# One bf16 mask for two uses, and f16 halves in the dense steps of x: a graph network kernel of two layers

## The reference, cut to what matters

```python
# x: 4096 x 256 f32, adj: 4096 x 4096 int32 (about 0.2% ones), neigh: 4096 x 256
mask = adj > 0
# layer 0
agg = mask @ x / max(sum(mask, 1), 1)
out = relu(concat(x @ W_self + b_self, agg @ W_nb + b_nb) @ W_comb + b_comb)
x = layernorm(x + out)
# layer 1
neib_att = tanh(neigh @ Wn1 + bn1) @ Wn2 + bn2      # hidden width 32
value    = neigh @ Wv + bv                          # width 128
x_att    = tanh(x @ Wx1 + bx1) @ Wx2 + bx2
ws  = softmax(where(mask, leaky_relu(x_att @ neib_att.T, 0.01), -9e15), axis=1)
out = concat(x @ Wfx + bfx, ws @ value)
return layernorm(x + out)
```

## Time and profile before

| | |
|---|---|
| median of three runs | 796.03 us |
| profiled execution | 795.35 us, span 793.5 us |
| TensorE matmul / weight load busy | 761.6 us (96%) / 640.6 us (81%) |
| VectorE, ScalarE, GpSimd busy | 593.4 us (75%), 561.1 us (71%), 295.0 us (37%) |
| chain that ended last, by engine | TensorE 90%, VectorE 3%, ScalarE 3% |
| DMA, mean share of 16 engines | queue of SyncE 45.9% |
| mean granted clock of TensorE | 0.993 |

### The profile page before, as it was taken

The page is one execution under the profiler, slowest core; times in us unless marked ns, Lnnn a source line. Parts: engine busy times, 40 slices in busy tenths (PEclk is TensorE's granted clock), DMA queues, the critical chain, the costliest instruction groups (busy, mean ns, idle before and its releaser), DMA issues.

```text
span 793.5 us, 20199 instructions
## 1 busy us (share of the span) xinstructions
PE 761.6 (96%) x7440; PEld 640.6 (81%) x7440; DVE 593.4 (75%) x1481; ACT 561.1 (71%) x1046; POOL 295.0 (37%) x368
## 2 busy tenths in 40 slices
PE   5999979999999999999999999999999999999885
PEld 4565758888888888888888888888888888888664
DVE  4875467778777787777777777777777787877784
ACT  2454247777777778777777777777777777777995
POOL 0031433344444433333444444333334444443101
PEclk9989999999999999999999999999999999999999
DMA  8954754544544444545445445454455444420000
GB/s 270 356 134 109 197 141 139 147 123 139 125 136 140 131 133 135 127 138 147 130 133 145 122 134 142 126 141 123 133 146 140 128 141 129 132 61 16 14 9 14
DMA packets 107404, 103.64 MB, mean 131 GB/s; under 512 B 74665, under 2 KB 88873, under 8 KB 107305
## 3 DMA queue, kind: packets, MB, share of 16 engines
q1 hardware_dynamic: 106944, 102.33, 45.9%
q10 hardware_dynamic: 360, 0.01, 0.0%
HBM read 81.34 MB, written 4.19 MB: 108 GB/s over the span
## 4 chain that ended last, share of the span: by engine, by line
PE 90%; DVE 3%; ACT 3%; issue 2%; POOL 1%; DMA 1%; SPq 0%; POOLq 0%; ACTq 0%; DVEq 0%
PE ps_v L974 20%; PE ps_agg L940 13%; PE ps_agg L937 13%; PE ps_t L961 13%; PE ps_agg L992 7%; PE ps_s L952 7%; PE ps_x L1012 3%; PE ps_x L1009 2%; PE ps_s L851 2%; PE ps_v L859 2%; PE ps_x L1018 2%; PE ps_t L842 1%; PE ps_x L868 1%; PE ps_agg L982 1%; DVE late L623 1%
## 5 line engine op out<-in xcount | busy, mean ns | idle before, releaser
L762 ACT ACTIVATE score<-ps_s,sc 128x512 f32<-128x512 f32 x256 | 178.0, 695 | 93.9 <-PE ps_s L952 90.0
L937 PE MATMUL ps_agg<-x,mask_t 128*128 128x257 f16 x1024 | 240.5, 273 | 0.0
L623 DVE TENSOR_TENSOR late<-ps_t,late 128x512 f16<-128x512 f32 x256 | 174.5, 682 | 85.3 <-ACT late L775 85.1
L577 DVE CUSTOM_DVE_ANT_0 score<-score,bias 128x512 f32<-128x512 f32 x256 | 191.1, 747 | 60.2 <-ACT score L762 60.1
L940 PE MATMUL ps_agg<-x,mask_t 128*128 128x256 f16 x1024 | 235.4, 273 | 0.0
L974 PEld LDWEIGHTS ps_v<-v,late 128*128 128x128 f16 x3072 | 191.7, 98 | 47.5 <-DVE late L623 13.7
L974 PE MATMUL ps_v<-v,late 128*128 128x128 f16 x3072 | 213.6, 219 | 7.6 <-DVE late L623 6.6
L775 ACT CAST late<-ps_t 128x512 f16<-128x512 f32 x256 | 147.8, 577 | 15.9 <-PE ps_t L961 15.7
L961 PE MATMUL ps_t<-ident,score 128*128 128x128 f32 x1024 | 155.7, 275 | 2.0 <-ACT score L769 1.8
L769 ACT ACTIVATE score<-score,exp_bias 128x1024 f32<-128x1024 f32 x128 | 146.5, 1145 | 0.8 <-DVE exp_bias L586 0.7
L388 POOL TENSOR_SCALAR mv<-mv 128x1 f32<-128x1 f32 x32 | 8.5, 265 | 370.0 <-DVE mv L608 370.0
(11 more groups left out here) (108 smaller groups left out, 734.4 us busy)
## 6 DMA issues: line engine op xcount, KB each, us to landing
adj_sb<-in_adj_dram SPq DMA_DIRECT2D x128, 512.0 KB, 4.0
neigh_sb<-in_L_gnn_neigh_dram SPq DMA_DIRECT2D x8, 512.0 KB, 7.9
score<-in_x_dram SPq DMA_DIRECT2D x8, 512.0 KB, 9.5
x_in<-in_x_dram SPq DMA_DIRECT2D x32, 128.0 KB, 3.7
out_dram<-out_sb SPq DMA_DIRECT2D x32, 128.0 KB, 3.9
mask_t<-mask SPq DMA_TRANSPOSE x128, 2.4
bias<-in_L_gnn_W_comb_dram SPq DMA_DIRECT2D x1, 512.0 KB, 9.4
bias<-in_L_gnn_W_self_dram SPq DMA_DIRECT2D x1, 256.0 KB, 7.0
```

The lines of the kernel that those rows point to most:

```text
L577: dve.tensor_tensor_reduce(score[:, b % 2, part], score[:, b % 2, part], bias[:, b % BIAS_BUFS, part], 1.0, -3.0e38, ALU.add, ALU.max, par ...
L623: dve.tensor_tensor(p_lo[:, k % 2, :], ps_t[k % 2][:, :], p_hi[:, k % 2, :], ALU.subtract).then_inc(p_lo_made, 1)
L762: act.activation(score[:, b % 2, k * GW:(k + 1) * GW], ps_s[k % 2][:, :], ACT.Prelu, alpha=SLOPE, scale=score_scale).then_inc(leaky_made, 1)
L937: mm = pe.matmul(agg[:, 0:D + 1], mask_t8[:, b % 2, c // 2, c % 2, :], x16[:, c, 0:D + 1], start=(c == 0), stop=(c == NC - 1), skip_group_ ...
```

## The change

- One mask in bf16, four buffers, serves both uses: 1.0 where there is no edge and 1.5 x 2^-121 where there is one. The low byte of the second reads as 2.0 in fp8, that of the first as zero; masked_scores subtracts the mask from scores that are kept in a large unit (score_unit). exp takes that unit as a pointer scale. GpSimd's make_bias is gone.
- Each quarter of the transpose has twice the bytes, x rows are loaded singly, and mask_t has one buffer of the same size: a quarter's transpose waits for the aggregation of the same quarter of the block before. Masks are made in slots -6, -5, -2, -1 of a block.
- x1 is stored as two f16 halves (x1_high on ScalarE, x1_low on VectorE), wx1 and wfx too; hidden and fx are six f16 matmuls each, with 96 columns of weights for hidden (three copies of wx1). tanh is written twice (f32 and f16, 96 rows), tanh_low makes the low part, x_attention is one f16 matmul with 96 x 96 weights.
- The new steps take two slots, so scores, row_max, turn, weigh and layer1 stand two slots later. The weights are scaled and split on VectorE in slots 1 to 10.

```diff
-MASK_AT = -5
-BIAS_AT = 3
+MASK_SLOTS = (-6, -5, -2, -1)
@@
-HIDDEN_AT = 17
-XATT_AT = 18
-STACK_AT = 19
-SCORE_AT = 20
-ROW_MAX_AT = 28
-TURN_AT = 30
-WEIGH_AT = 31
-LAYER1_AT = 39
+X1_LOW_AT = 17
+HIDDEN_AT = 18
+TANH_AT = 19
+XATT_AT = 20
+STACK_AT = 21
+SCORE_AT = 22
+ROW_MAX_AT = 30
+TURN_AT = 32
+WEIGH_AT = 33
+LAYER1_AT = 41
@@
-        mask = sb("mask", [P, 2, N], U8)
-        bias = sb("bias", [P, BIAS_BUFS, N], BF16)
-        mask_t = sb("mask_t", [P, 2, NC // 2, P], BF16)
+        mask = sb("mask", [P, MASK_BUFS, N], BF16)
+        mask_t = sb("mask_t", [P, NC, P], BF16)
@@ turn_mask
-                at_least(sp, agg_done, NQ * (b - 2) + q + 1)
-                sp.dma_start_transpose(mask_t[:, b % 2, q * CQ:(q + 1) * CQ, :],
-                                       mask_pairs[:, b % 2, q * QW // 2:(q + 1) * QW // 2]).then_inc(mask_t_in[q], 16)
+                at_least(sp, agg_done, NQ * (b - 1) + q + 1)
+                sp.dma_start_transpose(mask_t[:, q * CQ:(q + 1) * CQ, :],
+                                       mask[:, b % MASK_BUFS, q * QW:(q + 1) * QW]).then_inc(mask_t_in[q], 16)
@@ make_mask
-                dve.tensor_scalar(mask[:, b % 2, q * QW:(q + 1) * QW], adj_sb[:, q, :], 0.0, float(EDGE),
-                                  ALU.is_gt, ALU.mult).then_inc(mask_made, 1)
+                dve.tensor_scalar(mask[:, b % MASK_BUFS, q * QW:(q + 1) * QW], adj_sb[:, q, :], 0.0, EDGE,
+                                  ALU.is_le, ALU.add).then_inc(mask_made, 1)
@@
-            def make_bias(b, q):
...
@@ masked_scores
-                dve.wait_ge(bias_made, NQ * b + k // 2 + 1)
-                dve.tensor_tensor_reduce(score[:, b % 2, part], score[:, b % 2, part], bias[:, b % BIAS_BUFS, part],
-                                         1.0, -3.0e38, ALU.add, ALU.max,
+                dve.wait_ge(mask_made, NQ * b + k // 2 + 1)
+                dve.tensor_tensor_reduce(score[:, b % 2, part], score[:, b % 2, part], mask[:, b % MASK_BUFS, part],
+                                         1.0, -3.0e38, ALU.subtract, ALU.max,
@@
+            def x1_low(b):
+                dve.wait_ge(x1_hi_made, b + 1)
+                dve.scalar_tensor_tensor(out=x1_t[:, 1, :], in0=ps_x[:, 0:D], scalar=X1_SCALE, in1=x1_t[:, 0, :],
+                                         op0=ALU.mult, op1=ALU.subtract).then_inc(x1_lo_made, 1)
+            def tanh_low(b):
+                dve.wait_ge(tanh_made, 2 * b + 2)
+                part = slice(2 * H, H3)
+                dve.tensor_tensor(tanh16[part, :], tanh32[part, :], tanh16[part, :],
+                                  ALU.subtract).then_inc(tanh_split, 1)
@@ exps
-                act.activation(part, part, ACT.Exp, bias=exp_bias[:, b % 2:b % 2 + 1],
+                act.activation(part, part, ACT.Exp, bias=exp_bias[:, b % 2:b % 2 + 1], scale=score_unit,
@@ x_tanh
-                act.activation(tanh_sb[:, :], ps_x[0:H, 2 * P:3 * P], ACT.Tanh,
-                               bias=bx1_sb[:, 0:1]).then_inc(tanh_made, 1)
+                for out in (tanh32, tanh16):
+                    act.activation(out[:, :], ps_x[0:H3, 2 * P:3 * P], ACT.Tanh, bias=bx1_sb[0:H3, 0:1],
+                                   scale=h1_inv[0:H3, :]).then_inc(tanh_made, 1)
@@ hidden_and_fx
-                for dc in range(DC):
-                    pe.matmul(ps_x[0:H, 2 * P:3 * P], wx1_sb[:, dc, :], x1_t[:, dc * P:(dc + 1) * P],
-                              start=(dc == 0), stop=(dc == DC - 1))
-                for dc in range(DC):
-                    mm = pe.matmul(ps_x[:, 3 * P:4 * P], x1_t[:, dc * P:(dc + 1) * P], wfx_sb[:, dc, :],
-                                   start=(dc == 0), stop=(dc == DC - 1))
+                for k, (dc, (w, r)) in enumerate(product(range(DC), HI_LO)):
+                    pe.matmul(ps_x[0:H3, 2 * P:3 * P], wx1_16[:, dc, w, :], x1_t[:, r, dc * P:(dc + 1) * P],
+                              start=(k == 0), stop=(k == 3 * DC - 1))
+                for k, (dc, (r, w)) in enumerate(product(range(DC), HI_LO)):
+                    mm = pe.matmul(ps_x[:, 3 * P:4 * P], x1_t[:, r, dc * P:(dc + 1) * P], wfx16[:, dc, w, :],
+                                   start=(k == 0), stop=(k == 3 * DC - 1))
@@ x_attention
-                pe.matmul(ps_x[0:H3, 0:P], wx2_sb[:, :], tanh_sb[:, :], start=True, stop=True).then_inc(xatt_done, 1)
+                pe.matmul(ps_x[0:H3, 0:P], wx2_16[:, :], tanh16[:, :], start=True, stop=True).then_inc(xatt_done, 1)
```

More of the change, by code:

```diff
@@ L1 @@
 from contextlib import ExitStack
+from itertools import product
 import concourse.bass as bass
@@ L6 @@
 F32, F16, BF16, F8 = mybir.dt.float32, mybir.dt.float16, mybir.dt.bfloat16, mybir.dt.float8e4
-I32, U32, U8 = mybir.dt.int32, mybir.dt.uint32, mybir.dt.uint8
+I32, U32 = mybir.dt.int32, mybir.dt.uint32
 ALU = mybir.AluOpType
@@ L28 @@
 X_ONE, X_LO = D, D + 2
-BIG = 2.0 ** 100
-EDGE, EDGE_F8 = 64, 2.0
+EDGE = 1.5 * 2.0 ** -121
+EDGE_F8 = 2.0
+SCORE_BITS = 33
+MIN_SCORE_UNIT = 2.0 ** 8
 SLOPE = 0.01
@@ L36 @@
 TINY = 2.0 ** -100
+X1_SCALE = 2.0 ** 8
 TR = 4
@@ L164, in gnn_kernel @@
         tops = sb("tops", [P, 2, NT], F32)
-        early = bias[:, :, :].rearrange("p a n -> p (a n)").bitcast(F32)
+        early = mask[:, 2:4, :].rearrange("p a n -> p (a n)").bitcast(F32)
         ws_raw = early[:, 0:512].rearrange("p (c n) -> p c n", c=DC)
+        b_wide = early[:, 0:512].rearrange("p (c n) -> p c n", c=2 * DC)
         wn_raw = early[:, 512:1024].rearrange("p (c n) -> p c n", c=DC)
@@ L346, in _ @@
             for s in range(0, SLOTS + 3):
[L347 to L352, removed]
+                for q, at in enumerate(MASK_SLOTS):
+                    if (d := due(s, at, 0)) and d[0] > 0:
+                        turn_mask(d[0], q)
+                        if d[0] + 1 < NB:
+                            load_adj(d[0] + 1, q)
                 if d := due(s, LAYER0_AT + 1, 0):
@@ new lines, in scale_x_attention @@
+                wide = wx2_16[:, :].rearrange("p (k h) -> p k h", k=3)
+                scale_link(dve.tensor_copy(wide, wx2_sb[0:H3, :].unsqueeze(1).broadcast_to((H3, 3, H))))
+                part = slice(H, 2 * H)
+                dve.tensor_tensor(wide[part], wx2_sb[part, :].unsqueeze(1).broadcast_to((H, 3, H)), wide[part],
+                                  ALU.subtract).then_inc(x1_w_split, 1)
+                dve.tensor_scalar(bx2_sb[:, :], bx2_sb[:, :], s_xn[:, 0:1], None, ALU.mult).then_inc(bounds_scaled, 1)
@@ new lines, in split_fx, with split_wx1 @@
+            def split_fx():
+                scale = w_scale[:, 0:1]
+                scale_link(dve.tensor_scalar(wfx16[:, :, 0, :], wfx_sb[:, :, :], scale, None, ALU.mult))
+                dve.scalar_tensor_tensor(out=wfx16[:, :, 1, :], in0=wfx_sb[:, :, :], scalar=scale, in1=wfx16[:, :, 0, :],
+                                         op0=ALU.mult, op1=ALU.subtract).then_inc(x1_w_split, 1)
+            def split_wx1(c):
+                scale = w_scale[:, 1:2]
+                wide = wx1_16[:, c].rearrange("p v (k h) -> p v k h", k=3)
+                thrice = wx1_sb[:, c, :].unsqueeze(1).broadcast_to((P, 3, H))
+                scale_link(dve.tensor_scalar(wide[:, 0], thrice, scale, None, ALU.mult))
+                dve.scalar_tensor_tensor(out=wide[:, 1], in0=thrice, scalar=scale, in1=wide[:, 0], op0=ALU.mult,
+                                         op1=ALU.subtract).then_inc(x1_w_split, 1)
@@ L568, in first_part @@
                     scale_x_attention()
+                if s == 3:
+                    x1_weight_bounds()
+                if s == 5:
+                    scale_x1_weights()
+                if s == 7:
+                    split_fx()
+                if s in (8, 10):
+                    split_wx1((s - 8) // 2)
                 if s == Z_BIAS_SLOT:
@@ L617, in add_fx @@
                 dve.wait_ge(resx_made, b + 1)
-                dve.tensor_tensor(res[:, b % RES_BUFS, 0:DV], ps_x[:, 3 * P:4 * P], res[:, b % RES_BUFS, 0:DV],
-                                  ALU.add).then_inc(res_made, 1)
+                dve.scalar_tensor_tensor(out=res[:, b % RES_BUFS, 0:DV], in0=ps_x[:, 3 * P:4 * P], scalar=fx_inv,
+                                         in1=res[:, b % RES_BUFS, 0:DV], op0=ALU.mult, op1=ALU.add).then_inc(res_made, 1)
             def p_low(b, k):
@@ L654, in _ @@
                     masked_scores(*d)
+                if d := due(s, X1_LOW_AT, 0):
+                    x1_low(d[0])
+                if d := due(s, TANH_AT, 0):
+                    tanh_low(d[0])
                 if d := due(s, LAYER1_AT - 1, 0):
@@ L665, in _ @@
                     add_fx(d[0])
-                if d := due(s, MASK_AT):
-                    if d[0] > 0 and d[1] % 2 == 0:
-                        make_mask(d[0], d[1] // 2)
+                for q, at in enumerate(MASK_SLOTS):
+                    if (d := due(s, at, 0)) and d[0] > 0:
+                        make_mask(d[0], q)
                 if d := due(s, TURN_AT):
@@ L788, in normalise2, with x1_high @@
```

(8 more changed lines are left out.)

112 lines of the change are left out of this document (64 added, 48 removed).

## The result

| | before | after |
|---|---|---|
| median of the runs | 796.0 us | 769.15 us (768.72 to 770.73) |
| ratio | 1 | 0.9658, interval 0.9642 to 0.9673 |
| profiled execution, span | 795.35, 793.5 us | 770.73, 768.9 us |
| one block of the loop | 21.753 us | 20.889 us |

The kernel became 3.4% faster.

The account below looks back on a forecast made before the run. TensorE was taken as the bound: 28 blocks x 0.66 = -18.5 us, with once-only terms +1.6, +1.2, -3.3 and +1.5, sums to -17.5. Forecast 778.5 us, range 767 to 792.

Parts of the forecast that it names:

- Removed work: TensorE, each block: dropping f32 hidden and fx saves 1.20 us and f32 x_attention 0.48, together 1.68.
- Added work: TensorE, each block: f16 matmuls for fx 0.34, hidden 0.50, x_attention 0.08; sum 0.92 us, between 0.73 and 1.11.
- The rival of cheap narrow loads: TensorE's loop: 96-column loads are cheap and nothing stalls, 28 x 0.95 = 26.6 us saved, total 770.5; chance 0.11.
- No gaps: TensorE, hidden's 96-column weights: no loss where the weight shape changes; bounds nothing to 0.36 us a block.
- The stall: TensorE before slot 1's weighing, waiting for p_low or layer1: 0.1 us a block, range 0 to 0.6.
- this chain as a rival: Slot 1's chain becomes the bound: stall 0.5 instead of 0.1 us a block, total 790; chance 0.13.
- The GpSimd pass is hidden in the steady part, so its removal brings nothing there: Steady loop: removing GpSimd's mask pass was given no gain.
- The mask write keeps its pace: VectorE's mask write, 0.70 us, keeps its shape with bf16 output; over 0.8 us would make the prediction wrong.
- the slower rival: VectorE's mask write slows with bf16 output, each taking 0.6 us more: total 812 us; chance 0.06.
- The hole at 102 us: Head, TensorE's wait for the mean: 2.4 us less stall plus half the clock's 1.7, together -3.3 us.
- The first transpose: Start of the run: doubled data lands later and stalls TensorE 0.7 to 1.9 us, taken as +1.2.
- The tail: After the last aggregate: two more slots +3.8 us, exp's pointer scale with the second tanh +1.5.

Follow-up runs that it names:

- experiment 1: The changed kernel with hidden, fx and x_attention back in f32, mask, slots and buffers as changed: 795.91 us, ratio to before 0.9971, block 21.842 us.
- 3 and 4: The changed kernel with hidden's weights at 32 and at 64 columns instead of 96 from block 1 on: 775.51 and 776.21 us.
- experiment 2: The changed kernel with a GpSimd pass over each mask quarter back in its old odd slots from block 1, result unused: 799.54 us, ratio to before 1.0025.
- experiment 9: The changed kernel with the unused GpSimd pass over all four mask quarters put in slot 2, behind norm2: 773.79 us, ratio to before 0.9709.
- experiment 5: The changed kernel run once more, unaltered: 769.33 us, ratio to before 0.9655, block 20.889 us.
- experiment 8: The changed kernel with a constant instead of a pointer scale in exp, which leaves out the masking: 765.42 us, ratio to before 0.9612.
- experiment 6: The changed kernel with row_scale one slot earlier, in VectorE's slot 7 ahead of the mask: 765.85 us, ratio to before 0.9609.

## Why the prediction was right, and where not

**Removed work, right.** With the dense steps in f32 the block is 0.953 longer (experiment 1 against after). The 1.68 read from the earlier trace rows less the 0.728 measured as added is 0.952.

**Added work, the term that was mis-sized.** The prediction put a matmul with 96 columns at 0.083, the middle between an f16 row and an f32 row; it starts its successor after 0.056, like one with 128. Seven of them are 0.19 too dear a block, 28 blocks 5.3 us, most of the 6.1. The rival of cheap narrow loads, given 0.11, had this term right. That it came within 1.4 us of the time is in part luck: it saves 26.6 in the loop where 24.6 came, and too little in the head. The load record is longer, 123 against 98 ns, but it lies behind the running matmul:

```profile
L1073 PEld LDWEIGHTS ps_x<-x_t,wx 128*96 128x96 f16 x192 | 14.4, 123 | 1.7 <-DVE x_t L657 1.4
L1076 PEld LDWEIGHTS ps_x<-wfx,x_t 128*128 128x128 f16 x192 | 12.1, 98 | 0.0
```

TensorE: Matmul & The Clock Gate in the Trainium skill, Weight-path perf modes, keeps the fast load for 128 columns. The record agrees, the pace doesn't show it.

**No gaps, right**, and experiments 1, 3 and 4 show what they would have cost.

**The stall, right in size, wrong in place.** 0.1 was taken and 0.096 came, but not before slot 1's weighing. The size is partly luck: it was a guess in a range of 0 to 0.6. The argument from the earlier trace rows followed VectorE alone and stopped at layer1; the chain goes on through ScalarE's exp to slot 2's turn. The prediction named this chain as a rival at 0.5 of stall. It was right that it is the next bound: experiment 2 shows it at 0.92.

**"The GpSimd pass is hidden in the steady part, so its removal brings nothing there": failed.** It was true of the kernel before, where TensorE never waits, and experiment 1, without the pass, gains nothing in the loop. In the new slots it is not: there the pass, at the places that experiment 2 gives it, costs 0.92. The prediction had one half of the reason in hand. It moved hidden out of slot 1 and found the 1.20 us of cover gone, but it did not ask what the pass would cost there, and so what its removal is worth, nor what norm2's move would do to the order on GpSimd. In the new slots neither part was worth much without the other (795.91 us without the f16 products, 799.54 with the pass); together they are worth 27 us. That the whole 27 would have been missed with make_bias itself in the new slots is not shown, since the stand-in need not wait as make_bias did.

**The mask write keeps its pace, right:** 702 ns on average, so the slower rival had no ground.

```profile
L486 DVE TENSOR_SCALAR mask<-adj_sb 128x1024 bf16<-128x1024 int32 x128 | 89.6, 702 | 1.1 <-issue 0.2
L622 DVE CUSTOM_DVE_ANT_0 score<-score,mask 128x512 f32<-128x512 f32 x256 | 176.2, 688 | 18.7 <-ACT score L822 17.2
```

The mean of masked_scores fell from 747 to 688 ns: the ones that met a pass are gone.

**The hole at 102 us, right, and too cautious.** The wait is 0.78 instead of 2.94, 2.2 for the 2.4 taken. The granted clock from 100 to 120 us went from 0.91 to 1.00 altogether, where the prediction gave back one half of 1.7. The stretch also holds the dense steps of two blocks, which the sum left out: with f32 products it is 0.65 longer (experiment 1, 67.39 us against 66.74).

```profile
102.40 0.44 PE L1046 MATMUL ps_agg<-ident,mean 128*128 128x128 f32 x2 [0.78 <-ACT mean L812]
```

Experiment 9 brings the wait and the clock of 0.91 back with the passes alone.

**The first transpose, a term of +1.2 that came by luck.** Landing took 3.2 us instead of 2.5, so 0.7 more. But the 1.12 of the profiled execution are for the most part a first mask that was ready 1.00 us later (issue at 46.31 instead of 45.31). In experiment 5, the same kernel, the issue is at 44.98 and the first aggregate at 48.21, without a wait. From issue to first aggregate it is 3.09 before, 3.21 after and 3.23 there, so the doubled transpose costs 0.12 to 0.14 of the 1.2. Why the first mask comes sooner or later is open.

**The tail, right in sum.** In the tail 5.5 came for 5.3, in other parts: taking the exps' pointer away gives 0.8 (experiment 8), where 1.5 stood for them and tanh, and moving row_scale gives 1.5 (experiment 6), which the prediction did not see. The two were not tried together, so their sum is open.

## What to carry to other kernels

When a change moves or shortens work on the engine that sets the pace, ask again of every "hidden" step on the other engines whether it is hidden in the new schedule, and above all where it stands: a pass on GpSimd cost 0.02 us a block behind the long chain and 0.92 in front of it. Moving one product by a slot took 1.2 us of cover from the chain, and moving a small step by two slots changed what ran beside what on another engine. Follow such a chain over all engines until it meets the pacing engine; here its last link was an exp on ScalarE. Small operations that stand in the order ahead of a chain and are not needed yet are the cheapest thing to move: one line gave 0.45%. And hold a term that comes once against a second profile of the same kernel before calling it right.

## What the runs showed of the hardware

- An f16 matmul of 128 columns with a 96-column weight goes at 0.056 us, as one with 128; with 32 or 64 columns about 0.1 us is lost on the way in and again on the way out.
- The transpose of 128x1024 16-bit elements takes SyncE hardly longer to issue than that of half the size (1.23 against 1.19 us as the median), though the prediction allowed a doubling. It is the landing that grew: from 2.5 to 3.2 us for the first one, and over the whole run from a median of 2.4 (2.4 to 5.1) before to 4.2 after:

```profile
46.31 1.35 SPq L323 DMA_TRANSPOSE mask_t<-mask  x1
```

```profile
DMA to landing us min/median/max: 3.0/4.2/6.7
```

- A VectorE tensor_scalar and a GpSimd tensor_scalar on SBUF hardly overlap: the mask write takes 1.52 (experiment 2) and 1.58 us (experiment 9) instead of 0.68 beside passes of 1.05 to 1.5.
